# One core: batch 0's narrowing steps signalled singly from GpSimd, and a new order of the work on four engines

## The chip, the cores and the metric

One core of a Trainium2 chip runs one launch of the kernel. The metric is the device time of the launch in microseconds, lower is better. The engines are TensorE (PE), VectorE (DVE), ScalarE (ACT), GpSimd (POOL) and SyncE (SP, which issues transfers); each takes its own queue of instructions in order, and they meet only at semaphores.

## The reference

```python
# x: (4, 256, 256), ctx_512: (4, 256, 64)
def attention(h, x_normed, Wq, Wk, gamma_raw):           # h = ctx_512
    sim = einsum('bhnd,bhmd->bnm', heads(h @ Wq.T), heads(h @ Wk.T)) / (sqrt(16) * 4)
    threshold = top_k(sim, 76)[0][:, :, -1:]             # 76 = int(256 * 0.3)
    A = sigmoid(sim) * (sim >= threshold)
    A = (A + swapaxes(A, -1, -2)) * 0.5
    gamma = sigmoid(gamma_raw)
    return (1 - gamma) * x_normed + gamma * A

def ffn(x):                                              # rows of 256, 8 experts, 2 a row
    w, idx = top_k(softmax(x @ gate_w.T), 2)
    y = sum over the two experts: w * ((silu(x @ w1.T) * (x @ w3.T)) @ w2.T)
    z = (silu(x @ ws1.T) * (x @ ws3.T)) @ ws2.T          # shared expert
    return y + z

x = x + attention(ctx_512, layernorm(x), Wq, Wk, gamma_raw)
x = x + ffn(layernorm(x))
```

All is float32. Every expert is computed for every row; the routing weight of an expert that a row does not take is zero.

## The kernel before

The four batches (b = 0 to 3) of 256 rows are handled one after the other as two tiles of 128 partitions. For each batch there is an attention part and an expert part, and the experts come in five slots: slot 0 is the shared expert, slots 1 to 4 hold two experts each. Weights and activations are split into a high and a low part, and each product is three passes (high by high, high weight by low, low by high).

The attention part of a batch: TensorE makes queries and keys (`project`, L1282) and the scores (`similar`, L1299). The 76th largest score of each row is narrowed down by counting: a pivot is guessed from mean and deviation, the scores above it are counted, and the pivot is moved by a step in proportion to the count, twice. For batch 0 the left column of tiles is narrowed by VectorE (`narrow0`, L909) and the right one by ScalarE (`lean_first`, `lean_second`, `lean_last`, L654 to L677); GpSimd makes the step sizes and start values (`spans0`, L384). For batches 1 to 3 GpSimd makes them (`steps`, L394) and ScalarE counts (`first_balance`, `second_balance`, `last_pivot`). Then VectorE counts once more (`count_above`), removes what is above (`drop_above`), takes the next 16 values (`take_near`), picks the threshold and masks (`select`, L989). GpSimd says for each row whether the threshold lies within the 16 (`find_hits`, L417), TensorE sums this (`sum_hits`, L1308) and VectorE reads it (`read_hits`). TensorE transposes the masked scores (`transpose_masked`, L1317), VectorE adds (`residual1`, L1046), and the second layer norm is `norm2` on GpSimd (L433), then `norm2_first` on VectorE for batch 0 or `normed2` on ScalarE for the others; `transpose_z` (TensorE), `high_z` (ScalarE) and `low_z` (VectorE) make the two halves of the normed rows.

The expert part of slot s: `up` (L1379, TensorE) into two PSUM banks in turn, `silu` (ScalarE), `gate_values` (VectorE), `gate` with the routing weights (GpSimd, L443), `high_g` (ScalarE), `low_g` (VectorE), `down` (TensorE). `logits`, `route_a`, `tanh_logits`, `route_b` give the routing weights, and SyncE spreads them over all partitions through memory (`spread_gates`, L310). `up_lo` and `dn_lo`, the low parts of the weights, are made once, in the time of batch 0, by `lower_up` and `lower_down`, on GpSimd or for slots 1 and 3 on VectorE.

`keep_warm(n)` (L1276) issues n products of a tile of ones on TensorE, whose result nobody reads; each leaves two records in the trace. They stand in TensorE's queue between steps of batch 0, so that step and filler run in the order written. The order of every engine's work is written out by hand at the end of its block (L489 to L542 GpSimd, L726 to L820 ScalarE, L1168 to L1272 VectorE, L1454 to L1529 TensorE). Each engine stops at the first instruction whose semaphore is not there, whatever stands behind it.

## Time and profile before

| what | value |
|---|---|
| time, median of 3 runs | 113.38 us (113.3 to 114.48) |
| span of the profiled execution, first to last instruction | 111.5 us |
| median less that span | 1.88 us |
| TensorE busy | 102.9 us, 92% |
| VectorE busy | 84.4 us, 76% |
| GpSimd busy | 70.4 us, 63% |
| ScalarE busy | 61.7 us, 55% |
| share of TensorE in the chain that ended last | 78% |

The page of the profile gives the span of its own execution and no separate time for it; what lies around the span (start and end of the launch) is the third row of the table, if that execution was a middling one. Records of TensorE are pipelined, so the distance between the starts of two records says what one costs, and the length of one record is more than that. In a timeline, the note in brackets gives the idle time of the engine ahead of a row and who ended it; a row without one began as the engine came free.

### The profile page before, as it was taken

What the parts mean: (1) busy time and instruction counts of PE and PEld (TensorE: products, weight loads), DVE (VectorE), ACT (ScalarE), POOL (GpSimd) and SP (SyncE); (2) the same over time, 40 slices, a digit from 0 to 9 for tenths busy, and PEclk for the clock granted to TensorE, in tenths of its full rate; (3) what the DMA queues carried; (4) which work ended last, traced back from release to release, by engine and by line L of the source; (5) the groups of instructions that cost most, each with busy time, mean ns of one, the idle gap of its engine ahead of it and who ended that gap; (6) DMA issues with size and microseconds to landing.
All of it is one profiled execution on the core that took longest, in us unless ns stands there. A gap on an engine that the chain in (4) does not pass through costs nothing.

```text
span 111.5 us, 2502 instructions
## 1 busy us (share of the span) xinstructions
PE 102.9 (92%) x816; PEld 100.5 (90%) x816; DVE 84.4 (76%) x276; ACT 61.7 (55%) x155; POOL 70.4 (63%) x141
## 2 busy tenths in 40 slices
PE   6899709889999999999999999999999999999990
PEld 6699608778999999999999999999999999999990
DVE  6689899899998789867659979759418979365731
ACT  4179999989669856289691245243513352052400
POOL 4047788894975887899898591697028550465500
PEclk9999997699999999999999999999999999999999
DMA  2699995000003700000029000010483004520002
GB/s 40 135 341 370 343 374 163 3 0 3 0 0 96 281 9 0 3 0 6 3 47 309 21 9 0 32 62 0 111 263 104 6 3 154 228 94 0 0 0 94
DMA packets 8158, 10.33 MB, mean 93 GB/s; under 512 B 1936, under 2 KB 6544, under 8 KB 8144
## 3 DMA queue, kind: packets, MB, share of 16 engines
q1 hardware_dynamic: 7776, 10.13, 28.6%
q8 instruction: 6, 0.10, 0.4%
q10 hardware_dynamic: 368, 0.04, 0.3%
q14 instruction: 8, 0.07, 0.2%
HBM read 9.09 MB, written 1.08 MB: 91 GB/s over the span
## 4 chain that ended last, share of the span: by engine, by line
PE 78%; POOL 8%; DVE 5%; ACT 4%; issue 2%; POOLq 0%
PE ps_h L1407 23%; PE ps_u L1407 22%; PE ps_y L1435 20%; PE ps_a L1435 3%; PE ps_c L1354 3%; PE ps_u L1280 3%; ACT qkT L577 2%; PE ps_b L1337 1%; DVE near L970 1%; PE ps_a L1325 1%; PE ps_h L1289 1%; POOL rs L371 1%; DVE st L870 1%; DVE left L962 1%; DVE z L1060 1%
## 5 line engine op out<-in xcount | busy, mean ns | idle before, releaser
L452 POOL TENSOR_TENSOR gc<-prod,weights 128x512 f32<-128x512 f32 x16 | 25.9, 1634 | 15.3 <-DMA weights<-gates 9.3
L699 ACT ACTIVATE sil<-ps_h 128x512 f32<-128x512 f32 (+1 forms) x20 | 10.9, 552 | 16.1 <-PE ps_h L1407 16.1
L710 ACT ACTIVATE g_hi<-gc 128x512 fp32r<-128x512 f32 x16 | 10.1, 630 | 15.9 <-POOL gc L452 15.9
L1435 PE MATMUL ps_y<-dn_hi,g_hi 128*128 128x256 f32 x63 | 17.9, 284 | 0.0
L1435 PE MATMUL ps_y<-dn_hi,g_lo 128*128 128x256 f32 x63 | 17.7, 281 | 0.0
L1435 PE MATMUL ps_y<-dn_lo,g_hi 128*128 128x256 f32 x63 | 17.7, 281 | 0.0
L1136 DVE TENSOR_TENSOR g_lo<-gc,g_hi 128x512 fp32r<-128x512 f32 x16 | 13.8, 862 | 2.5 <-ACT g_hi L710 2.1
L1407 PE MATMUL ps_h<-z_hi,up_hi 128*128 128x256 f32 x70 | 14.7, 291 | 0.0
L1124 DVE TENSOR_TENSOR prod<-sil,ps_u 128x512 f32<-128x512 f32 x16 | 10.8, 679 | 4.9 <-ACT sil L699 3.2
L1407 PE MATMUL ps_h<-z_hi,up_lo 128*128 128x256 f32 x70 | 14.0, 281 | 0.0
L1407 PE MATMUL ps_u<-z_hi,up_hi 128*128 128x256 f32 x70 | 14.0, 281 | 0.0
L1407 PE MATMUL ps_h<-z_lo,up_hi 128*128 128x256 f32 x70 | 14.0, 281 | 0.0
L1407 PE MATMUL ps_u<-z_hi,up_lo 128*128 128x256 f32 x70 | 14.0, 281 | 0.0
L1407 PE MATMUL ps_u<-z_lo,up_hi 128*128 128x256 f32 x70 | 14.0, 281 | 0.0
L1280 PE MATMUL ps_u<-ones 128*128 128x128 f32 x72 | 12.5, 321 | 1.0 <-POOL ones L457 1.0
L1280 PEld LDWEIGHTS ps_u<-ones 128*128 128x128 f32 x72 | 11.8, 234 | 1.5 <-POOL ones L457 1.0
L1435 PEld LDWEIGHTS ps_y<-dn_lo,g_hi 128*128 128x128 f32 x63 | 11.9, 189 | 0.0
L1435 PEld LDWEIGHTS ps_y<-dn_hi,g_lo 128*128 128x128 f32 x63 | 11.9, 188 | 0.0
L1435 PEld LDWEIGHTS ps_y<-dn_hi,g_hi 128*128 128x128 f32 x63 | 11.9, 188 | 0.0
L1407 PEld LDWEIGHTS ps_h<-z_lo,up_hi 128*128 128x128 f32 x70 | 10.7, 188 | 0.0
L1407 PEld LDWEIGHTS ps_u<-z_lo,up_hi 128*128 128x128 f32 x70 | 10.7, 188 | 0.0
L1407 PEld LDWEIGHTS ps_u<-z_hi,up_lo 128*128 128x128 f32 x70 | 10.7, 188 | 0.0
(210 smaller groups left out, 250.3 us busy)
## 6 DMA issues: line engine op xcount, KB each, us to landing
weights<-gates SPq DMA_DIRECT2D x8, 512.0 KB, 4.5
x_sb<-in_x SPq DMA_DIRECT2D x4, 256.0 KB, 6.0
up_raw<-in_w1t SPq DMA_DIRECT2D x4, 256.0 KB, 5.9
up_raw<-in_w3t SPq DMA_DIRECT2D x4, 256.0 KB, 6.0
dn_raw<-in_w2t SPq DMA_DIRECT2D x4, 256.0 KB, 6.2
out_x<-fin SPq DMA_DIRECT2D x3, 256.0 KB, 2.1
out_x<-fin SPq DMA_DIRECT2D x2, 128.0 KB, 1.7
ctx_sb<-in_ctxT SPq DMA_DIRECT2D x1, 192.0 KB, 4.6
```

Of the source, the lines that this page charges most:

```text
L371: link(nc.gpsimd.tensor_tensor(rs1[:, :], var1[:, :], minus_half[:, :], ALU.pow))
L452: nc.gpsimd.tensor_tensor(gc[k % 2][:, :].rearrange("p (n t q) -> p n t q", n=2, t=T), prod[s][:, :].rearrange("p (n t q) -> p n t q", n=2 ...
L577: nc.scalar.activation(qkT[b][0:DC, a, :], ps_qk[b][a * DC:(a + 1) * DC, 0:N], ACT.Copy)\
L699: nc.scalar.activation(sil[i % 2][:, :w], ps_h[i % 2][:, :w], ACT.Silu).then_inc(silu_ready, 1)
L710: nc.scalar.activation(g_hi[s][:, :], src[:, :], ACT.Copy).then_inc(ghi0_ready if s == 0 else ghi_ready, 1)
L870: nc.vector.bn_stats(st0[0][:, t, :], ps_first[t][:, 0:N]).then_inc(first_stats, 1)
L1124: nc.vector.tensor_tensor(dst[:, :w], sil[i % 2][:, :w], ps_u[i % 2][:, :w], ALU.mult).then_inc(prod_ready, 1)
L1136: nc.vector.tensor_tensor(g_lo[s][:, :], src[:, :], g_hi[s][:, :].bitcast(F32), ALU.subtract).then_inc(glo0_ready if s == 0 else glo_ready, 1)
L1280: nc.tensor.matmul(ps_u[1][:, 0:P], ones[:, :], ones[:, :], start=True, stop=True)
L1354: last = nc.tensor.matmul(ps_c[:, t * 2 * E:(t + 1) * 2 * E], zz[b % 2][:, k, t * P:(t + 1) * P], gate_r[:, k, :, :].rearrange("p a e -> p ...
L1407: last = nc.tensor.matmul(dst, w[:, e, a, k, :], zz[b % 2][:, k, :], start=(m == 0), stop=(m == 3 * KD - 1))
L1435: last = nc.tensor.matmul(dst[:, t * D:(t + 1) * D], g[s][:, tok], w[:, e, :], start=(s == 0 and first and m == 0), stop=(s == SLOTS - 1 a ...
```

## The change

GpSimd's `spans0` issues the shift of the first step ahead of everything else, and each of three results raises `span_ready` by one: `from_a`, `from_b`, `step_b`. VectorE and ScalarE wait for the count that they need at each use, where before they waited once for the whole. Beside it the written order of all four engines is new. VectorE does both narrowing steps ahead of `gamma_parts` and `norm1(1)`; after `add_masked0` it takes `residual1(0)`, `score_stats(2)` and `norm2_first` ahead of `lower_up(1, 0)`. GpSimd does `lower_up(0, 1)`, `norm2(0)`, `steps(2)` and `find_hits(1)` ahead of `lower_down(0)` and `lower_gate`, and puts `lower_up(4, 0)` and `(4, 1)` ahead of `norm2(1)`. TensorE does `similar(3)` early, has longer stretches of `keep_warm` on either side of `transpose_masked(0)`, and takes `sum_hits(1)` behind `up(0, 1)`. A wait for `fin_ready` is put into `residual1(3)`. The diff, with later parts of the orders left out:

```diff
@@ -384,12 +385,14 @@
             def spans0():
 
                 pool.wait_ge(dev0_ready, 1)
+                nc.gpsimd.tensor_tensor(shifted_a[:, :], dev[0][:, :], shift_a[:, :], ALU.mult).then_inc(shifted_ready, 1)
                 nc.gpsimd.tensor_tensor(step_a[:, :], dev[0][:, :], scale_a[:, :], ALU.mult)
-                nc.gpsimd.tensor_tensor(step_b[:, :], dev[0][:, :], scale_b[:, :], ALU.mult)
-                nc.gpsimd.tensor_tensor(shifted_a[:, :], dev[0][:, :], shift_a[:, :], ALU.mult)
-                link(nc.gpsimd.tensor_tensor(shifted_b[:, :], dev[0][:, :], shift_b[:, :], ALU.mult))
-                nc.gpsimd.tensor_tensor(from_a[:, :], shifted_a[:, :], mv0[0][:, :, 0], ALU.add)
+                nc.gpsimd.tensor_tensor(shifted_b[:, :], dev[0][:, :], shift_b[:, :], ALU.mult).then_inc(shifted_ready, 1)
+                pool.wait_ge(shifted_ready, 1)
+                nc.gpsimd.tensor_tensor(from_a[:, :], shifted_a[:, :], mv0[0][:, :, 0], ALU.add).then_inc(span_ready, 1)
+                pool.wait_ge(shifted_ready, 2)
                 nc.gpsimd.tensor_tensor(from_b[:, :], shifted_b[:, :], mv0[0][:, :, 0], ALU.add).then_inc(span_ready, 1)
+                nc.gpsimd.tensor_tensor(step_b[:, :], dev[0][:, :], scale_b[:, :], ALU.mult).then_inc(span_ready, 1)
...
@@ -499,39 +502,39 @@
             find_hits(0)
             steps(1)
             norm1(1)
+            lower_up(0, 1)
+            norm2(0)
+            steps(2)
+            find_hits(1)
+            lower_up(2, 0)
+            lower_up(2, 1)
             lower_down(0)
             lower_gate()
-            norm2(0)
-            find_hits(1)
-            lower_up(0, 1)
-            lower_up(2, 0)
-            lower_up(2, 1)
             add_masked(1)
-            steps(2)
-            norm2(1)
             lower_up(4, 0)
             lower_up(4, 1)
+            norm2(1)
             norm1(2)
+            lower_down(1)
+            steps(3)
+            find_hits(2)
             gate(0, 1)
-            find_hits(2)
             gate(0, 2)
-            gate(0, 3)
-            steps(3)
             add_masked(2)
-            lower_down(1)
             lower_down(2)
             norm2(2)
+            gate(0, 3)
             gate(0, 4)
             lower_down(3)
...
@@ -663,6 +666,7 @@
                 act.wait_ge(span_ready, 1)
                 nc.scalar.activation(aim1[:, 1:2], lean[:, 0:1], ACT.Identity, bias=from_a[:, 1:2],
                                      scale=step_a[:, 1:2]).then_inc(lean_aim_ready, 1)
+                act.wait_ge(span_ready, 2)
                 nc.scalar.activation(part0[:, 1:2], lean[:, 0:1], ACT.Identity, bias=from_b[:, 1:2],
                                      scale=step_a[:, 1:2]).then_inc(lean_part_ready, 1)
...
+                act.wait_ge(span_ready, 3)
                 nc.scalar.activation(pivot[0][:, 1:2], lean[:, 1:2], ACT.Identity, bias=part0[:, 1:2],
                                      scale=step_b[:, 1:2]).then_inc(lean_pivot_ready, 1)
...
@@ -725,9 +730,9 @@
 
             copy_q0()
             tanh_first()
+            tanh_gamma()
             copy_qk(1)
             copy_qk(2)
-            tanh_gamma()
             lean_first()
             copy_qk(3)
             lean_second()
@@ -735,81 +740,81 @@
             lean_last()
             copy_scores_summed()
             sigmoid(0)
-            upper_down(0)
-            sigmoid(1)
             upper_up(0, 1)
-            upper_gate()
             upper_up(1, 0)
             upper_up(1, 1)
+            copy_scores(2)
+            upper_down(0)
             first_balance(1)
             second_balance(1)
             last_pivot(1)
-            copy_scores(2)
-            upper_down(1)
+            copy_scores(3)
+            upper_gate()
+            high_z(0)
             upper_up(2, 0)
             upper_up(2, 1)
             upper_up(3, 0)
-            high_z(0)
-            copy_scores(3)
+            silu(0, 0)
...
@@ -913,12 +918,14 @@
                     dve.wait_ge(tanh_ready, 1)
                     link(count_first(0, aim0))
                     dve.wait_ge(span_ready, 1)
-                    nc.vector.tensor_scalar(part0[:, 0:1], count[:, 0:1], step_a[:, 0:1], from_b[:, 0:1],
+                    nc.vector.tensor_scalar(aim1[:, 0:1], count[:, 0:1], step_a[:, 0:1], from_a[:, 0:1],
                                             ALU.mult, ALU.add)
-                    link(nc.vector.tensor_scalar(aim1[:, 0:1], count[:, 0:1], step_a[:, 0:1], from_a[:, 0:1],
+                    dve.wait_ge(span_ready, 2)
+                    link(nc.vector.tensor_scalar(part0[:, 0:1], count[:, 0:1], step_a[:, 0:1], from_b[:, 0:1],
                                                  ALU.mult, ALU.add))
                 else:
                     link(count_first(0, aim1))
+                    dve.wait_ge(span_ready, 3)
                     link(nc.vector.tensor_scalar(pivot[0][:, 0:1], count[:, 0:1], step_b[:, 0:1], part0[:, 0:1],
                                                  ALU.mult, ALU.add))
 
...
                 dve.wait_ge(maskT_ready, b + 1)
                 dve.wait_ge(base_ready, b + 1)
+                if b >= 3:
+                    dve.wait_ge(fin_ready, T * (b - 2))
                 nc.vector.tensor_tensor(x1[b % 3][:, :, :], base[:, :, :],
                                         ps_a[:, :].rearrange("p (t n) -> p t n", t=T), ALU.add).then_inc(x1_ready, 1)
...
@@ -1170,10 +1179,10 @@
             first_score_stats()
             norm1(0)
             aims0()
+            narrow0(0)
+            narrow0(1)
+            gamma_parts()
             norm1(1)
-            narrow0(0)
-            gamma_parts()
-            narrow0(1)
             count_last0(0)
             count_last0(1)
             drop_above(0)
@@ -1182,88 +1191,88 @@
             take_near(0, 1)
             select(0)
             add_masked0()
+            residual1(0)
+            score_stats(2)
+            norm2_first()
             lower_up(1, 0)
-            residual1(0)
+            count_above(1)
+            low_z(0)
             lower_up(1, 1)
-            count_above(1)
-            norm2_first()
             drop_above(1)
             take_near(1, 0)
+            gate_values(0, 0)
             take_near(1, 1)
+            lower_up(3, 0)
+            gate_values(0, 1)
             read_hits(1)
-            low_z(0)
             select(1)
-            score_stats(2)
-            route_a(0)
-            gate_values(0, 0)
-            residual1(1)
-            low_g(0, 0)
-            route_b(0)
-            gate_values(0, 1)
-            lower_up(3, 0)
             lower_up(3, 1)
             norm1(2)
+            gate_values(0, 2)
+            residual1(1)
+            route_a(0)
+            route_b(0)
+            low_g(0, 0)
+            score_stats(3)
+            gate_values(0, 3)
             low_z(1)
-            gate_values(0, 2)
-            score_stats(3)
-            route_a(1)
-            gate_values(0, 3)
+            gate_values(0, 4)
             count_above(2)
-            gate_values(0, 4)
             drop_above(2)
             take_near(2, 0)
             gate_values(1, 0)
-            low_g(0, 1)
+            norm1(3)
             take_near(2, 1)
             read_hits(2)
...
@@ -1458,64 +1467,60 @@
             keep_warm(1)
             project(1)
             project(2)
+            project(3)
             keep_warm(1)
-            project(3)
-            keep_warm(6)
             similar(1)
             similar(2)
+            similar(3)
             keep_warm(7)
             sum_hits(0)
-            keep_warm(2)
+            keep_warm(15)
             transpose_masked(0)
-            keep_warm(1)
-            similar(3)
-            keep_warm(7)
-            sum_hits(1)
-            keep_warm(1)
+            keep_warm(16)
             transpose_z(0)
             keep_warm(3)
             up(0, 0)
+            up(0, 1)
+            sum_hits(1)
+            up(0, 2)
             logits(0)
-            keep_warm(1)
             transpose_masked(1)
-            up(0, 1)
-            up(0, 2)
+            up(0, 3)
+            up(0, 4)
+            transpose_z(1)
             down(0, 0)
-            transpose_z(1)
-            up(0, 3)
+            up(1, 0)
             logits(1)
-            up(0, 4)
-            up(1, 0)
             up(1, 1)
             sum_hits(2)
             up(1, 2)
             transpose_masked(2)
             up(1, 3)
-            down(0, 1)
             up(1, 4)
             transpose_z(2)
+            down(0, 1)
...
```

## Rows read from the trace of the kernel before

**Rows 1.** Windows view: busy time of each engine, granted clock, DMA, by stretch.
```profile
18.00:19.00 1.00, 1.00 (x4) 0.81 (x3) 0.98 (x2) 1.00 (x5) 0.85 (x3) 0.50 0.06 19
...
26.10:60.00 33.90, 33.88 (x289) 33.88 (x290) 27.61 (x105) 25.02 (x64) 27.38 (x51) 1.00 0.16 46
60.00:109.00 49.00, 48.95 (x415) 48.75 (x414) 34.08 (x94) 15.77 (x30) 25.35 (x25) 1.00 0.22 73
```

**Rows 2.** Timeline of TensorE, 0 to 36 us: start, length, line, out<-in, count.
```profile
7.80 1.50 PE L1280 MATMUL ps_u<-ones 128*128 128x128 f32 x12
9.13 1.03 PE L1304 MATMUL ps_b<-qkT 128*128 128x256 f32 x4
...
13.52 0.69 PE L1280 MATMUL ps_u<-ones 128*128 128x128 f32 x4
16.97 0.63 PE L1325 MATMUL ps_a<-ident,masked 128*128 128x128 f32 x4 [2.76 <-DVE looked L1035]
...
19.12 2.77 PE L1280 MATMUL ps_u<-ones 128*128 128x128 f32 x14
22.82 0.35 PE L1314 MATMUL ps_a<-hit,ones 128*128 128x2 f32 x2 [0.93 <-POOL hit L424]
...
23.34 0.60 PE L1337 MATMUL ps_b<-ident,z 128*128 128x128 f32 x4
...
24.63 0.51 PE L1374 MATMUL ps_h<-z_hi,up_hi 128*128 128x256 f32 x2
...
26.12 0.51 PE L1374 MATMUL ps_h<-z_lo,up_hi 128*128 128x256 f32 x2 [0.28 <-DVE z_lo L1066]
```

**Rows 3.** Timeline of ScalarE, 0 to 45 us.
```profile
11.28 0.37 ACT L676 ACTIVATE pivot<-lean,part,step_b 128x1 f32<-128x1 f32 x1
...
20.39 0.63 ACT L584 ACTIVATE scores<-ps_h 128x256 f32<-128x256 f32 x2
```

**Rows 4.** Timeline of VectorE, 0 to 45 us.
```profile
11.69 0.48 DVE L906 TENSOR_SCALAR_CACHE_REDUCE over<-ps_y,pivot 128x256 f32<-128x256 f32 x1 [0.43 <-ACT pivot L676]
...
17.70 0.68 DVE L859 TENSOR_TENSOR up_lo<-up_raw,up_hi 128x512 fp32r<-128x512 f32 x1
18.30 0.68 DVE L1050 TENSOR_TENSOR x<-base,ps_a 128x512 f32<-128x512 f32 x1
...
19.80 0.25 DVE L839 BATCH_NORM_AGGREGATE mv<-st 128x2 f32<-128x6 f32 x2
...
21.84 0.74 DVE L1060 TENSOR_SCALAR z<-x,mv,rs 128x256 f32<-128x256 f32 x2 [0.36 <-POOL rs L437]
```

**Rows 5.** Timeline of GpSimd, 0 to 60 us, batch 0.
```profile
8.73 0.20 POOL L392 TENSOR_TENSOR from_b<-shifted_b,mv 128x2 f32<-128x2 f32 x1
...
19.95 0.76 POOL L364 TENSOR_TENSOR gate_r<-gate_sb,gate_r 128x16 fp32r<-128x16 f32 x1
...
21.09 0.71 POOL L437 TENSOR_TENSOR rs<-var,minus_half 128x2 f32<-128x2 f32 x1
```

**Rows 6.** Chain that ended last, 26 to 36 us: start, length, what.
```profile
28.41 1.42 PE ps_h L1407 x12
```

**Rows 7.** Timeline of GpSimd, 0 to 60 us, batch 1's second norm and what stands near it.
```profile
27.48 1.29 POOL L430 TENSOR_TENSOR base<-ln,masked 128x512 f32<-128x512 f32 x1 [1.64 <-DVE looked L1035]
...
31.39 0.33 POOL L435 TENSOR_SCALAR var<-mv 128x2 f32<-128x2 f32 x1
...
34.84 2.55 POOL L351 TENSOR_TENSOR up_lo<-up_raw,up_hi 128x512 fp32r<-128x512 f32 x2 [1.73 <-ACT up_hi L555]
```

**Rows 8.** Timeline of ScalarE, 0 to 45 us, batch 1's normed rows.
```profile
33.14 1.09 ACT L683 ACTIVATE z<-x,nb,rs 128x256 f32<-128x256 f32 x2 [0.18 <-POOL nb L441]
```

**Rows 9.** Timelines of GpSimd (0 to 60 us) and of VectorE (44 to 112 us).
```profile
45.01 1.61 POOL L452 TENSOR_TENSOR gc<-prod,weights 128x512 f32<-128x512 f32 x1 [1.06 <-DVE g_lo L1136]
...
46.36 0.31 DVE L975 SCALAR_TENSOR_TENSOR kth_pick<-above,count,near 128x16 f32<-128x16 f32 x1
...
46.60 0.22 DVE L975 SCALAR_TENSOR_TENSOR kth_pick<-above,count,near 128x16 f32<-128x16 f32 x1
```

More of the change, by code:

```diff
@@ L532, in _ @@
             gate(1, 3)
+            norm2(3)
             gate(1, 4)
-            norm2(3)
             gate(2, 1)
@@ L1215, in _ @@
             gate_values(1, 0)
-            low_g(0, 1)
+            norm1(3)
             take_near(2, 1)
@@ L1222, in _ @@
             residual1(2)
+            route_a(1)
             route_b(1)
+            low_g(0, 1)
             low_g(0, 2)
+            low_z(2)
+            count_above(3)
             gate_values(1, 3)
-            low_z(2)
-            norm1(3)
             gate_values(1, 4)
+            drop_above(3)
+            take_near(3, 0)
             low_g(1, 0)
             low_g(0, 3)
+            gate_values(2, 0)
+            low_g(0, 4)
             route_a(2)
-            count_above(3)
-            low_g(0, 4)
-            drop_above(3)
-            take_near(3, 0)
-            gate_values(2, 0)
-            gate_values(2, 1)
-            take_near(3, 1)
-            low_g(1, 1)
-            read_hits(3)
-            low_g(1, 2)
-            select(3)
-            residual2(0)
+            take_near(3, 1)
+            read_hits(3)
+            residual2(0)
+            select(3)
+            low_g(1, 1)
+            gate_values(2, 1)
             gate_values(2, 2)
             residual1(3)
+            low_g(1, 2)
+            route_b(2)
+            low_z(3)
             low_g(1, 3)
-            route_b(2)
+            gate_values(2, 3)
             low_g(1, 4)
-            gate_values(2, 3)
+            route_a(3)
             gate_values(2, 4)
-            low_z(3)
+            residual2(1)
             low_g(2, 0)
-            residual2(1)
             gate_values(3, 0)
-            route_a(3)
+            route_b(3)
             low_g(2, 1)
-            route_b(3)
             low_g(2, 2)
@@ L1260, in _ @@
             low_g(2, 4)
+            low_g(3, 0)
             gate_values(3, 1)
-            low_g(3, 0)
             gate_values(3, 2)
-            residual2(2)
             low_g(3, 1)
             low_g(3, 2)
+            residual2(2)
             gate_values(3, 3)
@@ L1493, in _ @@
             up(1, 3)
-            down(0, 1)
             up(1, 4)
             transpose_z(2)
+            down(0, 1)
             down(0, 2)
+            logits(2)
             up(2, 0)
-            logits(2)
             up(2, 1)
```

77 lines of the change are left out of this document (39 added, 38 removed).

## The prediction

> **What bounds the kernel now.** I read the windows first, because the busy shares of the whole span hide two different stages. From 26.1 to 109 us TensorE is busy in all but 0.07 of 82.9 us at the full clock [rows 1]: there nothing but TensorE's own work counts, as long as the other engines keep ahead of it. So a change of order can win only by letting that stretch begin sooner, and it can lose by opening holes in it. Next the timeline of TensorE shows what the stretch waited for [rows 2]. The transposes of batch 0's normed rows start at 23.34, the first product of `up(0, 0)` at 24.63, and its third pass at 26.12, behind `low_z(0)`. Last come the timelines of the engines that feed these three points [rows 3 to 5].
>
> **The narrowing, signalled singly.** Before, the single signal comes with `from_b` at 8.93 [rows 5]; now `from_a` signals ahead of it, by a few tenths. VectorE also does its two narrowing steps ahead of `norm1(1)`. But both columns have to be there before the scores of batch 0 are sorted out, and the right column belongs to ScalarE: VectorE sat idle for 0.43 us ahead of its count of that column, and ScalarE's pivot at 11.28 to 11.65 ended the wait [rows 3, 4]. ScalarE came to that pivot without an idle note, so it was late by its own queue; up to there the change only moves `tanh_gamma` in it, and the sum in front of the first lean count stays. VectorE's work ahead of that point is the same set in another order, so the 0.43 us cover the delay of `norm1(1)`; without them it would cost up to that. I book nothing, with bounds of -0.1 and +0.1 for two more waits in ScalarE's queue. The new wait in `residual1(3)` is for `residual2(0)`, earlier in VectorE's own queue: nothing.
>
> **Batch 0 from mask to normed rows.** Before, `lower_up(1, 0)` on VectorE, begun at 17.70 as `add_masked0` ended, kept `residual1(0)` back to 18.30 [rows 4]. It is now behind, so the residual starts near 17.72, as soon as the transposes are through (16.97 and 0.63 after it [rows 2]). From the residual's start to its last statistics took 20.05 - 18.30 = 1.75 us [rows 4], so these come at 19.47. On GpSimd `norm2(0)` began only once `lower_gate` ended at 20.71, and was done at 21.80 [rows 5]: 1.09 us. In the new order only `lower_up(0, 1)` stands ahead, in the place of `lower_down(0)` and of the same size, over about when `lower_gate` began, 19.95. I put `norm2(0)` at 19.75 to 19.95 and its end at 20.85 to 21.05, 0.75 to 0.95 us sooner. `norm2_first` took 0.74 [rows 4], so the normed rows are complete at 21.6 to 21.8; `score_stats(2)`, put in between, fills VectorE's wait.
>
> Before, this gain would have been lost: rows ready at 22.58 were transposed only at 23.34, since `sum_hits(1)` stood ahead in TensorE's queue and waited 0.93 us for GpSimd's hits [rows 2, 4]. That step now follows `up(0, 1)`. What stands ahead now is filler. A record of filler costs (9.13 - 7.80) / 12 = 0.111 us [rows 2]; 30 of them from 13.52 end at 16.85, just before the transposes of the mask (16.97). Four transposes and 32 records of filler more, at the same pitch, end at 20.97, before the rows are ready. So the filler is hidden, with 0.6 us to spare. `similar(3)`, moved early, is hidden too: TensorE idled between the early filler and the first hits.
>
> From the first of four transposes to `up(0, 0)` took 24.63 - 23.34 = 1.29 us; now two of the four are done while the second tile is normed, which saves 0.22. `up(0, 0)` starts at 21.6 + 1.07 = 22.67. ScalarE has both score copies of batches 2 and 3 ahead of `high_z(0)` now, about 1 us each by the two halves in [rows 3] and a tanh; they sit in its queue near 16 and 21, and I estimate that it is free at 21.7, before it is needed at 22.05. The third pass follows 26.12 - 24.63 - 0.28 = 1.21 us after the start, the wait taken off [rows 2], at 23.88. It needs `low_z(0)`: VectorE has `lower_up(1, 0)` and `count_above(1)` between, together 1.5 us (from 20.0, the end of the statistics, to 21.48, where the idle note of the 21.84 row begins [rows 4]); 21.55 + 1.5 + 0.68 for a product of 128x512 gives 23.7, or 0.3 later if GpSimd's `steps(2)` gets in between. So the third pass runs at 23.88 to 24.1 instead of 26.12: 2.0 to 2.25 us. One filler goes out of the full stretch and `sum_hits(1)` comes in, each two records: nothing. I take 2.25.
>
> **What the full stretch gives back.** Two places in the new order look too tight.
>
> First, `transpose_z(1)`. A pair of `up` costs 2.84 us (twice the piece in [rows 6]). TensorE has up(0, 0) done at 24.4, two pairs, a sum, the logits and the mask's transposes till 31.7, then two pairs, and wants batch 1's normed rows at 37.3. `residual1(1)` cannot start before 31.8. With 1.75 us for it and 34.23 - 31.39 = 2.84 us from GpSimd's `norm2(1)` to the end of ScalarE's rows [rows 7, 8] they could be there at 36.4. But GpSimd now has `add_masked(1)` (1.29) and `lower_up(4, 0)` and `(4, 1)` (2.55 [rows 7]) ahead of `norm2(1)`. If these begin only with the mask, near 31.0, `norm2(1)` starts at 34.8 and the rows end at 37.7; if a microsecond later, at 38.7. The stall is 0 to 1.4, and I take 0.3, near the first case.
>
> Second, `select(2)`. `gate(0, 2)` now stands immediately ahead of `add_masked(2)` on GpSimd, which waits for `select(2)`, and batch 0's routing weights come later, as `route_b(0)` moved behind `residual1(1)`. So GpSimd's two long products (1.61 us each) fall on the time when VectorE picks the threshold of batch 2, with small instructions that read two operands. The first `kth_pick` at 46.36, begun while a gate ran to 46.62, took 0.31 and not 0.22 [rows 9]. So the price lies between nothing and one whole gate, 1.6 us; how the two meet I can place only to a microsecond. I take 0.6, nearer the row, which lost 0.09. The Trainium skill, page "SBUF — State Buffer", section "Who interferes with whom", says that a VectorE instruction with two SBUF inputs contends with a GpSimd instruction that reads SBUF, and that the later one blocks until the other is through. The row agrees, since only the last 0.26 us of the gate were left; taken at the row's 0.09 this place would leave the time at 111.5, by the rule at its worst at 113.0. It reaches TensorE whole, since `transpose_masked(2)` stands in its queue with `up(1, 3)` behind.
>
> Sum: 2.25 - 0.3 - 0.6 = 1.35 us. The span goes from 111.5 to 110.15; with the same 1.88 around it, 112.0 against the median of 113.38.
>
> **Rivals.** (a) No hole opens: 113.38 - 2.25 = 111.1. For it speak the slack that the other engines have (VectorE is busy 27.6 of 33.9 us, GpSimd 27.4 [rows 1]); against it, both places above. (b) The holes eat the gain: both at the upper bound, 1.4 + 1.6 = 3.0, gives 114.1; the middle of both, 1.5, gives 112.6, and a third hole of half a microsecond in a queue where every order is new gives 113.1. For it: GpSimd's chain from the mask to the normed rows of batch 1 is longer by two products. (c) Slower: the filler runs at half clock. From 18 to 19 the granted clock was 0.50, the 1.2 GHz level, after TensorE had idled 2.76 us [rows 1, 2], and 14 records took 2.77 us, 0.198 each. The new filler lies on the path. If only the second block (32 records) runs so, it ends 2.8 us later, at 23.8, and `up(0, 0)` starts at about 25: near no change. If the clock falls before the mask's transposes, 30 records more cost 2.6 us and the third pass comes at about 29.2: 116.4. Whether the clock falls before 16.97 decides. Against it: the idle time ahead that let it fall is filled. (d) The change misses its own aim, since the narrowing's gain ends at ScalarE: that is in my sum already, and costs nothing.
>
> **How the numbers follow.** Of changes here, 1% (1.1 us) is about what a measurement tells from none. The forecast, holes of some 0.5 to 1.1 us in all: 0.37. (a): 0.19. (b): 0.33, within 1% for nearly all. (c) slow: 0.07, and 0.04 for holes above 3.4 us. So faster 0.56, same 0.33, slower 0.11. The range of the likeliest alone is 111.7 to 112.3; with (a) below it and (b) up to 113.9 it is 110.9 to 113.9, which leaves out (c) and a lucky start.
>
> **What would show it.** VectorE still waits for ScalarE's pivot near 11.65; `norm2_first` near 20.9 and `up(0, 0)` near 22.7, with the third pass on its heels; granted clock 1.00 from 13 to 21; TensorE's waits list a normed row or a copy of batch 1 near 37 and the mask of batch 2 near 47, a few tenths each; the end of TensorE's work about 1.35 us sooner. I am wrong if `up(0, 0)` starts at 24 or later, if the holes sum to over 1.5 us, or if filler is what TensorE ends last before a transpose.

## The result: 0.6% faster, half of what was forecast

The changed kernel takes 113.32 us in the median of 20 executions (112.47 to 114.84) against 113.56 us for the kernel before (113.3 to 114.5, 20 executions). The ratio is 0.9943, 95% interval 0.9918 to 0.9969: 0.65 us less of 113.56, with 0.35 to 0.93 inside the interval. The ratio leaves out the five longest executions of the changed kernel (114.32 us and above) as slow ones, which is one reason why it says more than the two medians; over all 20 the means are 113.50 and 113.78, 0.28 us apart. The forecast was 1.35 us less, so the time falls into "within 1%". The direction is right and the size is not.

Four views show where the 0.65 us come from. First the windows of the changed kernel, with the columns of [rows 1]; the second one begins with the third pass of `up(0, 0)`:

```profile
18.00:19.00 1.00, 1.00 (x11) 0.98 (x11) 0.89 (x3) 1.00 (x6) 0.92 (x2) 1.00 0.12 43
25.02:60.00 34.98, 34.62 (x288) 33.65 (x287) 31.84 (x118) 26.81 (x67) 28.39 (x46) 1.00 0.09 32
```

The granted clock at 18 to 19 us, 0.50 before [rows 1], is now 1.00. But the full stretch, idle for 0.02 us of 33.9 before [rows 1], now has 34.98 - 34.62 = 0.36 us of idle time in its first half (none from 60 to 109). Records of TensorE that wait for an operand also count as busy, so the timeline shows more (start, length, line, out<-in, count; compare [rows 2]):

```profile
18.07 0.63 PE L1334 MATMUL ps_a<-ident,masked 128*128 128x128 f32 x4
18.54 3.74 PE L1289 MATMUL ps_u<-ones 128*128 128x128 f32 x32
22.61 0.67 PE L1346 MATMUL ps_b<-ident,z 128*128 128x128 f32 x4 [0.34 <-DVE z L1069]
...
25.02 0.39 PE L1383 MATMUL ps_h<-z_lo,up_hi 128*128 128x256 f32 x2
...
38.39 0.84 PE L1346 MATMUL ps_b<-ident,z 128*128 128x128 f32 x4
39.00 0.36 PE L1444 MATMUL ps_y<-dn_hi,g_hi 128*128 128x256 f32 x1
...
39.92 0.50 PE L1416 MATMUL ps_h<-z_hi,up_hi 128*128 128x256 f32 x2
...
40.64 0.51 PE L1416 MATMUL ps_h<-z_lo,up_hi 128*128 128x256 f32 x2
...
49.02 0.63 PE L1334 MATMUL ps_a<-ident,masked 128*128 128x128 f32 x4 [0.36 <-DVE looked L1042]
49.61 0.47 PE L1416 MATMUL ps_h<-z_hi,up_hi 128*128 128x256 f32 x2
```

The last two rows have these for counterparts in the kernel before:

```profile
48.97 0.60 PE L1325 MATMUL ps_a<-ident,masked 128*128 128x128 f32 x4
49.32 0.48 PE L1407 MATMUL ps_h<-z_hi,up_hi 128*128 128x256 f32 x2
```

The reader is to see three things. The filler is out of the way before each group of transposes: what ends the wait at 22.61 is VectorE's normed row, and at 18.07, where no wait is noted, the transposes follow VectorE's last step of the mask by 0.22 us (17.85), as they do in e6 with a third of the filler. The third pass stands at 25.02, not at 23.88 as forecast. And the two holes are there, each where it was expected. At 38.39 the transposes of batch 1 take 0.61 us to the next start, where batch 3's, unstalled, took 0.36 (76.50 to 76.86), and the passes at 39.92 and 40.64 are late as well. At 49.02 the mask of batch 2 is waited for, and the step behind its transposes comes after 0.59 us, where it came after 0.35 before.

The timelines of VectorE and GpSimd in the same execution, which answer to [rows 4, 5, 7]:

```profile
9.70 0.27 DVE L921 TENSOR_SCALAR aim<-count,step_a,from_a 128x1 f32<-128x1 f32 x1
...
12.78 0.48 DVE L911 TENSOR_SCALAR_CACHE_REDUCE over<-ps_y,pivot 128x256 f32<-128x256 f32 x1 [0.23 <-ACT pivot L681]
...
22.06 0.73 DVE L1069 TENSOR_SCALAR z<-x,mv,rs 128x256 f32<-128x256 f32 x2 [0.39 <-POOL rs L440]
...
29.79 0.20 DVE L993 TENSOR_SCALAR hits<-ps_a 1x1 int32<-1x1 f32 x1
...
30.74 0.88 DVE L987 SCALAR_TENSOR_TENSOR masked<-scores,kth,sig 128x256 f32<-128x256 f32 x2 [0.45 <-DVE kth_pick L982]
...
35.17 0.25 DVE L844 BATCH_NORM_AGGREGATE mv<-st 128x2 f32<-128x6 f32 x2
...
46.22 1.56 DVE L982 SCALAR_TENSOR_TENSOR kth_pick<-above,count,near 128x16 f32<-128x16 f32 x1
...
48.78 0.68 DVE L1133 TENSOR_TENSOR prod<-sil,ps_u 128x512 f32<-128x512 f32 x1
...
81.27 0.95 DVE L1092 TENSOR_TENSOR lgd<-lgx,lg 128x16 f32<-128x16 f32 x1
82.15 0.15 DVE L1094 COPY take<-lg 128x4 f32<-128x4 f32 x1
```
```profile
33.34 2.57 POOL L352 TENSOR_TENSOR up_lo<-up_raw,up_hi 128x512 fp32r<-128x512 f32 x2
36.00 0.22 POOL L438 TENSOR_SCALAR var<-mv 128x2 f32<-128x2 f32 x1
...
44.49 3.25 POOL L455 TENSOR_TENSOR gc<-prod,weights 128x512 f32<-128x512 f32 x2
```

Batch 1's statistics were there at 35.42, but GpSimd's `norm2(1)` began at 36.00, behind the two products of `lower_up(4, *)`. The first `kth_pick` of batch 2 took 1.56 us (0.31 in [rows 9], and 0.22 for the second one there): it began during `gate(0, 2)` and ended with it, at 47.7. The row at 48.78 is `gate_values(1, 1)`, behind the masks in VectorE's queue.

For the comparison of several kernels I read the starts of a few steps from TensorE's timeline of each. The columns: from the first scores to the sum of batch 0's hits; from there to the third pass of `up(0, 0)`; from the transposes of batch 1's normed rows to its logits; from there to the mask transposes of batch 2; from there to batch 2's logits; from the logits of batch 3 to TensorE's end; from the third pass to the end (us; of before, whose order is another, the first two and the last).

| kernel | scores to hits | hits to pass | norm 1 to logits 1 | to mask 2 | to logits 2 | logits 3 to end | pass to end |
|---|---|---|---|---|---|---|---|
| before | 8.19 | 12.81 | | | | | 82.84 |
| changed | 9.13 | 10.62 | 3.31 | 7.32 | 9.62 | 29.45 | 84.21 |
| e1_same | 8.96 | 10.63 | 3.28 | 7.34 | 9.62 | 30.23 | 84.97 |
| e2_one_signal | 9.43 | 10.61 | 3.29 | 7.32 | 9.61 | 29.45 | 84.15 |
| e3_gate_behind | 9.10 | 10.62 | 3.29 | 6.79 | 10.18 | 29.45 | 84.27 |
| e4_read_early | 8.21 | 10.62 | 3.06 | 7.21 | 9.61 | 29.99 | 84.41 |
| e5_norm2_late | 8.54 | 11.31 | 3.29 | 7.38 | 9.62 | 29.45 | 84.27 |
| e6_little_filler | 8.88 | 11.06 | 3.30 | 7.36 | 9.61 | 29.64 | 84.53 |
| e7_batch3 | 8.19 | 10.62 | 3.28 | 7.36 | 9.61 | 29.45 | 84.19 |
| e8_best | 8.23 | 10.63 | 3.52 | 6.93 | 9.62 | 29.44 | 84.06 |
| e9_product_early | 8.20 | 10.64 | 3.06 | 7.72 | 9.62 | 29.45 | 84.34 |
| e11_two_edits | 8.19 | 10.62 | 3.06 | 7.16 | 9.61 | 29.45 | 83.78 |

The first column is not the change's: it differs between executions of one order (e4, e7 and e11 have the changed order up to there and 8.19 to 8.21, as before; the changed kernel itself 9.13 and 8.96). The second column is the gain, 12.81 - 10.62 = 2.19; it is 10.61 to 10.64 in every execution but those of e5 and e6, whose edits lie in it. The last is the loss, 84.21 - 82.84 = 1.37, and 2.13 in the second execution.

### The profile page after: what moved, and what is told of

Same layout as the page of the kernel before. It is cut to its first block, busy times and chain, and to the rows that moved or that the text cites. A ratio compares the mean times of both kernels' runs of the same rounds, so it can differ in the third digit from the quotient of the medians.

```text
span 111.8 us, 2555 instructions
## 1 busy us (share of the span) xinstructions
PE 106.6 (95%) x842; PEld 102.9 (92%) x842; DVE 83.0 (74%) x276; ACT 61.4 (55%) x155; POOL 71.9 (64%) x141
## 3 DMA queue, kind: packets, MB, share of 16 engines
HBM read 9.09 MB, written 1.08 MB: 91 GB/s over the span
## 4 chain that ended last, share of the span: by engine, by line
PE 74%; POOL 10%; DVE 8%; issue 5%; ACT 1%; DVEq 0%; POOLq 0%
PE ps_h L1416 20%; PE ps_y L1444 19%; PE ps_u L1416 19%; PE ps_a L1444 3%; PE ps_u L1289 3%; PE ps_c L1363 2%; PE ps_b L1346 2%; PE ps_a L1334 1%; POOL up_lo L352 1%; PE ps_h L1298 1%; PE ps_c L1305 1%; DVE near L977 1%; PE ps_h L1383 1%; DVE ps_b L900 1%; POOL rs L372 1%
## 5 line engine op out<-in xcount | busy, mean ns | idle before, releaser
L455 POOL TENSOR_TENSOR gc<-prod,weights 128x512 f32<-128x512 f32 x16 | 27.0, 1708 | 16.6 <-DMA weights<-gates 8.1
L1145 DVE TENSOR_TENSOR g_lo<-gc,g_hi 128x512 fp32r<-128x512 f32 x16 | 12.3, 781 | 8.2 <-ACT g_hi L715 8.1
L1289 PE MATMUL ps_u<-ones 128*128 128x128 f32 x98 | 13.9, 296 | 1.0 <-POOL ones L460 1.0
L1289 PEld LDWEIGHTS ps_u<-ones 128*128 128x128 f32 x98 | 13.4, 211 | 1.4 <-POOL ones L460 1.0
L1416 PEld LDWEIGHTS ps_h<-z_hi,up_hi 128*128 128x128 f32 x70 | 10.7, 189 | 0.3 <-ACT z_hi L696 0.2
L1416 PEld LDWEIGHTS ps_u<-z_hi,up_hi 128*128 128x128 f32 x70 | 10.7, 188 | 0.0
```

What stands on the lines that cost most here:

```text
L455: nc.gpsimd.tensor_tensor(gc[k % 2][:, :].rearrange("p (n t q) -> p n t q", n=2, t=T), prod[s][:, :].rearrange("p (n t q) -> p n t q", n=2 ...
L1145: nc.vector.tensor_tensor(g_lo[s][:, :], src[:, :], g_hi[s][:, :].bitcast(F32), ALU.subtract).then_inc(glo0_ready if s == 0 else glo_ready, 1)
L1289: nc.tensor.matmul(ps_u[1][:, 0:P], ones[:, :], ones[:, :], start=True, stop=True)
L1416: last = nc.tensor.matmul(dst, w[:, e, a, k, :], zz[b % 2][:, k, :], start=(m == 0), stop=(m == 3 * KD - 1))
```

## The experiments

Each is an edit of the changed kernel; the ratio is to the kernel before on the same chip. Only e5 and e10 have intervals clear of the unchanged order's 0.9918 to 0.9969, so what the other edits do is read from the rows and columns, with the ratio beside it.

**e1_same: the changed kernel once more.**

> The changed kernel once more, as it is, for a second trace. In the first trace the first scores of batch 0 took 1.19 us a pair where they took 0.67 before, and all of batch 0 came some 1.1 us late behind them. Theory: that is the clock of the first microseconds, which differs from execution to execution and not with the change. Then this trace may show the pair at 0.67 again, and if so the third pass of up(0, 0) comes at about 23.9, the span is about 110.7, and the holes near 38 to 41 us (0.5) and 48 to 50 us (0.6) stand as before, 1 us sooner. Rival: the new order makes the front late. Then the pair takes 1.19 again and the third pass comes at 25.0 again. Time against the kernel before: 0.990 to 0.997 by both.

Measured 113.5 us, ratio 0.995 (0.9917 to 0.9984): the result stands. Its trace shows a hole that the first one had not. VectorE, GpSimd and TensorE:

```profile
80.92 1.60 DVE L1092 TENSOR_TENSOR lgd<-lgx,lg 128x16 f32<-128x16 f32 x1
82.44 1.69 DVE L1094 COPY take<-lg 128x4 f32<-128x4 f32 x1
```
```profile
80.84 3.27 POOL L455 TENSOR_TENSOR gc<-prod,weights 128x512 f32<-128x512 f32 x2 [4.63 <-DMA weights<-gates]
```
```profile
85.28 0.47 PE L1416 MATMUL ps_h<-z_hi,up_hi 128*128 128x256 f32 x2 [0.54 <-DVE prod L1133]
```

`route_a(3)` on VectorE meets two of GpSimd's gates back to back. Here the first gate keeps `lgd` back for 1.60 us and the second one the copy for 1.69; in the execution above `lgd` took 0.95 and the copy got in between the gates, 0.15. `gate_values(2, 4)` stands behind, and TensorE's `up(3, 1)` waits for it. The hole is 30.23 - 29.45 = 0.78 us here, 0 in the other one.

**e2_one_signal: the old single signal in the new order.**

```diff
-  shifted_a.then_inc(shifted_ready) ... from_a.then_inc(span_ready), from_b.then_inc(span_ready), step_b.then_inc(span_ready)
+  step_a, step_b, shifted_a, link(shifted_b), from_a, from_b.then_inc(span_ready)      # and one wait for it
```

> The new order with the old signalling: spans0 signals once at its end, in its old sequence, and both narrowing engines wait for that. Theory: ScalarE's pivot ends the wait, VectorE had 0.23 us to spare in the changed kernel, and the single signal comes 0.3 to 0.45 later; so VectorE's last count comes at most 0.2 us later and the time is 0 to +0.2 us against the changed kernel, ratio to the kernel before 0.993 to 0.997. Rival: the single signals are what the change gains from; then the ratio is 1.00.

113.91 us, ratio 0.9988 (0.9954 to 1.0023). VectorE waits for the signal now:

```profile
10.04 0.27 DVE L916 TENSOR_SCALAR aim<-count,step_a,from_a 128x1 f32<-128x1 f32 x1 [0.54 <-POOL from_b L392]
```

It is at 10.04 where the changed kernel is at 9.70, 0.34 later with the scores 0.07 earlier. Everything behind in VectorE's queue is later too, `gamma_parts` with it, for which GpSimd waits ahead of the hits; the changed kernel and then this run (in the kernel before the wait was 0.18 us):

```profile
11.42 0.30 POOL L375 TENSOR_SCALAR c<-rs,g_rest 128x2 f32<-128x2 f32 x1 [0.43 <-DVE g_quarter L1174]
```
```profile
11.76 0.30 POOL L374 TENSOR_SCALAR c<-rs,g_rest 128x2 f32<-128x2 f32 x1 [0.73 <-DVE g_quarter L1167]
```

The first column is 9.43, against 8.88 to 9.13 in the four executions of the single signals whose first scores took as long. So in the new order the single signals are worth 0.3 us or more; the intervals of the two ratios overlap, and the rows carry this.

**e3_gate_behind: `gate(0, 2)` out of the pick's way.**

```diff
-  find_hits(2), gate(0, 1), gate(0, 2), add_masked(2)     # GpSimd
+  find_hits(2), gate(0, 1), add_masked(2), gate(0, 2)
-  gate_values(1, 2), residual1(2)                         # VectorE
+  residual1(2), gate_values(1, 2)
```

> gate(0, 2) behind add_masked(2) on GpSimd, and residual1(2) ahead of gate_values(1, 2) on VectorE. Theory: in the changed kernel the first pick of batch 2 took 1.56 us behind gate(0, 2) and TensorE stood 0.5 to 0.7 us for it. Without the gate there the pick takes 0.22, the hole near 49 us goes, and the time falls by 0.5 us against the changed kernel: ratio to the kernel before about 0.988 to 0.991. Rival: the hole is only moved, since gate(0, 2) and what waits for it come later; then the pick is short but the ratio stays at 0.994.

113.49 us, ratio 0.9948 (0.9913 to 0.9982): nothing gained. VectorE and GpSimd:

```profile
46.02 0.21 DVE L982 SCALAR_TENSOR_TENSOR kth_pick<-above,count,near 128x16 f32<-128x16 f32 x1
...
47.23 0.88 DVE L987 SCALAR_TENSOR_TENSOR masked<-scores,kth,sig 128x256 f32<-128x256 f32 x2 [0.83 <-DVE kth_pick L982]
```
```profile
49.55 1.65 POOL L455 TENSOR_TENSOR gc<-prod,weights 128x512 f32<-128x512 f32 x1
...
52.53 0.23 POOL L438 TENSOR_SCALAR var<-mv 128x2 f32<-128x2 f32 x1
```

The pick is free and the mask 0.53 us sooner (6.79 for 7.32), so the gate was what blocked it, and TensorE no longer waits for the mask. But `norm2(2)` now stands behind the gate, and batch 2's logits come 0.56 later: the hole has moved. The row at 47.23 shows a floor under it: between the sum of the hits at 45.90 and the masks lie 1.33 us, in which VectorE's queue reads the sum back for its branch.

**e4_read_early: the same read-back, for batch 1, ahead of a product.**

```diff
-  lower_up(3, 0), gate_values(0, 1), read_hits(1), select(1)     # VectorE
+  lower_up(3, 0), read_hits(1), gate_values(0, 1), select(1)
```

> read_hits(1) ahead of gate_values(0, 1) on VectorE, nothing else. Theory: in the changed kernel the masks of batch 1 began 0.95 us after read_hits(1) began, with 0.45 us of idle time, as they did for batch 2 in the kernel before, since the hits are read back into VectorE's queue; that kept add_masked(1), both lower_up(4) and norm2(1) on GpSimd late, which made the hole at 38 to 41 us. With the read 0.6 us earlier the idle time goes, norm2(1) comes 0.3 to 0.45 us sooner, that hole shrinks by 0.3: ratio to the kernel before about 0.991. Rival: norm2(1) is held by batch 1's own statistics on VectorE; then GpSimd waits for them and the hole stays.

113.05 us, ratio 0.9911 (0.9877 to 0.9945). In the changed kernel the masks of batch 1 come 0.95 us after `hits` with 0.45 of idle time; here the product of 0.67 lies in that time, the masks follow the picks with no wait, and the third column falls by 0.25. This execution has the hole of e1, the third one, at 0.54.

**e5_norm2_late: one product back ahead of batch 0's norm.**

```diff
-  lower_up(0, 1), norm2(0), ..., lower_up(2, 1), lower_down(0), lower_gate()     # GpSimd
+  lower_up(0, 1), lower_down(0), norm2(0), ..., lower_up(2, 1), lower_gate()
```

> The changed kernel with lower_down(0) put back ahead of norm2(0) on GpSimd, nothing else. My account of the front: norm2(0) ends the wait for batch 0's normed rows, so one product of 0.73 us ahead of it reaches TensorE whole: from the first scores to the third pass of up(0,0) 19.5 us at a cold first pair (18.8 at a warm one in the run with the early read) becomes 20.3 (19.6), and the ratio to the kernel before goes from 0.995 to 1.001. Rival: the front is bound by something else by now (the filler, ScalarE's copies, low_z), and the segment does not grow by more than 0.2 us.

114.24 us, ratio 1.0025 (0.9988 to 1.0062). TensorE waits for the normed row 0.70 longer, and the second column is 11.31 for 10.62, the 0.72 us of the product:

```profile
22.58 0.67 PE L1346 MATMUL ps_b<-ident,z 128*128 128x128 f32 x4 [1.04 <-DVE z L1069]
```

So what stands ahead of `norm2(0)` on GpSimd reaches TensorE one to one. The rest of the 2.19 us (`sum_hits(1)` out of TensorE's way, the residual ahead of `lower_up(1, 0)`) no run tested by itself.

**e6_little_filler: the filler cut from 31 products to 10.**

```diff
-  keep_warm(15), transpose_masked(0), keep_warm(16)     # TensorE
+  keep_warm(2),  transpose_masked(0), keep_warm(8)
```

> The changed kernel with 2 and 8 filler products for 15 and 16 ahead of and behind the transposes of batch 0's mask. If the filler is only cover, as the prediction had it, the clock falls as it did in the kernel before (0.50 at 18 to 19 us), but is back before up(0,0), and the third pass comes within 0.2 us of where it came. The rival: up(0,0) and the transposes ahead of it then run at half the clock, some 12 records at twice 0.12 to 0.24 us, and the third pass comes 0.5 to 1.5 us later; then part of the front's gain is the filler's, and the ratio is 1.000 to 1.008.

113.41 us, ratio 0.993 (0.9893 to 0.9967). The windows and the timeline of TensorE:

```profile
18.00:19.00 1.00, 1.00 (x7) 1.00 (x6) 0.69 (x3) 1.00 (x6) 0.90 (x2) 0.50 0.31 107
...
23.00:24.00 1.00, 1.00 (x9) 0.98 (x7) 0.88 (x5) 0.68 (x2) 0.86 (x6) 0.73 0.05 16
```
```profile
17.63 1.08 PE L1334 MATMUL ps_a<-ident,masked 128*128 128x128 f32 x4 [2.76 <-DVE looked L1042]
18.51 3.62 PE L1289 MATMUL ps_u<-ones 128*128 128x128 f32 x16
```

After 2.76 us without work the granted clock is 0.50, the 1.2 GHz level, until 23; 16 records of filler take as long as 32 did. It is back before `up(0, 0)`, so of the work that counts only the transposes run slowly (1.08 us for four, where they took 0.63 to 0.67): the third pass comes 11.06 - 10.62 = 0.44 us later, between what the two sides expected. In the time it is not to be seen beside the unchanged order.

**e7_batch3: the third hole taken away.**

```diff
-  route_a(3), gate_values(2, 4)     # VectorE
+  gate_values(2, 4), route_a(3)
-  high_g(2, 1), silu(2, 4)          # ScalarE
+  silu(2, 4), high_g(2, 1)
```

> The changed kernel with gate_values(2,4) ahead of route_a(3) on VectorE and silu(2,4) ahead of high_g(2,1) on ScalarE. The account of the third hole: it opens in some executions, when route_a(3)'s small products are blocked by two gates of GpSimd back to back and keep gate_values(2,4) back. Then here it never opens: from the logits of batch 3 to the end 29.45 us, and the time is below the unchanged order's by the hole's 0.5 to 0.8 times its frequency, 0.2 to 0.4 us: ratio 0.991 to 0.993. Rival: the blocked product then keeps back low_g or the weights of batch 3 and the hole comes later: 29.9 or more, ratio 0.995.

113.08 us, ratio 0.9933 (0.9899 to 0.9967), and no hole (29.45). In this trace the copy was not blocked (0.16), but it was in e8, e10 and e11, which have the same edit (1.65 to 1.69), and TensorE did not wait for `gate_values(2, 4)` in any of them. With the hole shut, the columns give 2.19 - 1.35 = 0.84 us, a ratio of 0.9926 beside 0.9933 measured; against the unchanged order the intervals overlap.

**e8_best: the first hole attacked at its cause.**

```diff
-  lower_up(2, 1), lower_down(0), lower_gate(), add_masked(1), lower_up(4, 0), lower_up(4, 1), norm2(1)     # GpSimd
+  lower_up(2, 1), lower_up(4, 0), lower_gate(), add_masked(1), lower_up(4, 1), lower_down(0), norm2(1)
-  norm1(2), gate_values(0, 2), residual1(1)                                                                # VectorE
+  gate_values(0, 2), residual1(1), norm1(2)           # with the edits of e4 and e7
```

> All that the runs so far point to: read_hits(1) ahead of gate_values(0,1), the reorder of batch 3, and for the first hole lower_up(4,0) ahead of add_masked(1) in the place of lower_down(0), which goes ahead of norm2(1), with norm1(2) behind residual1(1) on VectorE. If the holes are what GpSimd's and VectorE's orders make, the stretch from the second norm's transposes to the logits of batch 1 shrinks from 3.3 to 2.6 us, from the third pass to the end 83.3 to 83.6 us where the changed kernel has 84.2 to 85.0, and the ratio is 0.982 to 0.988. The rival: closing a hole lets the next wait come up, as in the run that moved a gate; then no more than the early read's 0.991.

113.09 us, ratio 0.9927 (0.9895 to 0.996): no better than without it. The rows of batch 1 are in time, and another wait has come up behind them, for a product that `norm1(2)` pushed back; the third column is 3.52.

```profile
39.30 0.48 PE L1416 MATMUL ps_h<-z_hi,up_hi 128*128 128x256 f32 x2 [0.57 <-DVE prod L1133]
```

**e9_product_early: that product ahead of `score_stats(3)`.**

```diff
-  low_g(0, 0), score_stats(3), gate_values(0, 3), low_z(1)     # VectorE, on top of e8
+  low_g(0, 0), gate_values(0, 3), low_z(1), score_stats(3)
```

> The version with all edits, and gate_values(0,3) and low_z(1) ahead of score_stats(3) on VectorE. In that version the first hole had moved from batch 1's normed rows to up(1,0)'s wait of 0.57 us for gate_values(0,3), which norm1(2) had pushed back. If that product is the last thing in the way, the stretch from the second transposes of normed rows to the logits of batch 1 falls from 3.52 to 2.6 to 2.8 us, from the third pass to the end 83.2 to 83.5 us (84.06 before the edit, 84.2 in the changed kernel), ratio 0.984 to 0.988. Rival: batch 1's z_lo or the later steps(3), which wait for score_stats(3), take its place: 83.9 or more, ratio 0.991 to 0.994.

113.36 us, ratio 0.9966 (0.9932 to 1.0): no better. The third column is 3.06, but the fourth is 7.72: TensorE now waits 0.77 us for the mask of batch 2. VectorE and TensorE:

```profile
38.58 0.69 DVE L1075 TENSOR_TENSOR z_lo<-ps_b,z_hi 128x512 fp32r<-128x512 f32 x1 [0.34 <-ACT z_hi L696]
...
45.82 1.02 DVE L982 SCALAR_TENSOR_TENSOR kth_pick<-above,count,near 128x16 f32<-128x16 f32 x1
...
47.04 0.88 DVE L987 SCALAR_TENSOR_TENSOR masked<-scores,kth,sig 128x256 f32<-128x256 f32 x2
```
```profile
48.09 0.63 PE L1334 MATMUL ps_a<-ident,masked 128*128 128x128 f32 x4 [0.77 <-DVE looked L1042]
```

With nothing left between the product and `low_z(1)`, VectorE stands still for 0.34 us, and no other idle time of it is noted until the masks; it reads the hits at 45.70, in e8 at 45.26, with the third pass at 23.96 in both. A gate blocks the pick here too, but that costs nothing: the masks begin 1.22 us after the pick began, as in e10 below, where the pick is free.

**e10_gate_later: `gate(0, 2)` behind `norm2(2)`.**

```diff
-  gate(0, 2), add_masked(2), lower_down(2), norm2(2)     # GpSimd, on top of e9
+  add_masked(2), lower_down(2), norm2(2), gate(0, 2)     # high_g, low_g, down (0, 2) moved along; residual1(2) ahead of gate_values(1, 2)
```

> The version with the earlier product, and gate(0,2) moved behind norm2(2) on GpSimd, with what hangs on it on ScalarE, VectorE and TensorE moved along (high_g(0,2), low_g(0,2), down(0,2)). In the run that moved gate(0,2) only behind add_masked(2), the pick was free (0.21 us) but batch 2's norm waited for the gate. If the second hole is only this one gate, then from the logits of batch 1 to the logits of batch 2 the time falls by 0.5 to 0.6 us against the version without the move, and the ratio is 0.979 to 0.985. Rival: the read-back of the hits (0.95 to 1.33 us from read_hits to the masks) or the late down(0,2) keeps 0.3 us or more of it.

121.5 us, ratio 1.0674 (1.0624 to 1.0724). I had overlooked a buffer: the product of slot 2 of batch 1 overwrites what `gate(0, 2)` reads, so VectorE stops at `gate_values(1, 2)`, and with it all behind it. VectorE from the pick on:

```profile
46.07 0.21 DVE L982 SCALAR_TENSOR_TENSOR kth_pick<-above,count,near 128x16 f32<-128x16 f32 x1
...
47.29 0.88 DVE L987 SCALAR_TENSOR_TENSOR masked<-scores,kth,sig 128x256 f32<-128x256 f32 x2 [0.84 <-DVE kth_pick L982]
...
54.83 0.69 DVE L1133 TENSOR_TENSOR prod<-sil,ps_u 128x512 f32<-128x512 f32 x1 [3.33 <-POOL gc L455]
```

Up to the masks the move gained nothing either: the pick took 0.21 us for 1.02, but the read-back of the hits lies beside it, and from the logits of batch 1 to the mask transposes it is 7.72 us, as in e9. What the second hole is worth when it is shut and nothing else opens is therefore not measured.

**e11_two_edits: the edits of e4 and e7, nothing else.**

> The changed kernel with the early read of batch 1's hits and the reorder of batch 3, nothing else. If the gains add up, 0.2 to 0.35 us from the first and 0.2 to 0.4 us on the average from the second (the hole that opens in some executions), the ratio is 0.988 to 0.990, from the third pass to the end 83.8 to 83.9 us. Rival: the two share one stall, and the ratio is 0.993 as for the batch 3 edit alone.

112.31 us against 113.56 in five executions, ratio 0.9899 (0.9863 to 0.9934), the lowest found. The interval still holds the rival's 0.993; the columns show the two gains side by side (3.06, 29.45, and 83.78 from the pass to the end). VectorE at `route_a(3)`; then ScalarE, VectorE and TensorE around `up(1, 0)`:

```profile
79.98 1.63 DVE L1092 TENSOR_TENSOR lgd<-lgx,lg 128x16 f32<-128x16 f32 x1
81.53 1.65 DVE L1094 COPY take<-lg 128x4 f32<-128x4 f32 x1
```
```profile
38.14 0.60 ACT L696 ACTIVATE z_hi<-ps_b 128x512 fp32r<-128x512 f32 x1 [0.25 <-PE ps_b L1346]
```
```profile
38.77 0.69 DVE L1075 TENSOR_TENSOR z_lo<-ps_b,z_hi 128x512 fp32r<-128x512 f32 x1 [0.55 <-ACT z_hi L696]
```
```profile
38.80 0.50 PE L1416 MATMUL ps_h<-z_hi,up_hi 128*128 128x256 f32 x2
...
39.52 0.51 PE L1416 MATMUL ps_h<-z_lo,up_hi 128*128 128x256 f32 x2
```

Both small instructions of `route_a(3)` are blocked in full, as in e1, and no hole follows (29.45), since the product that TensorE wants stands ahead of them, at 78.88. The first pass of `up(1, 0)` begins as `high_z(1)` ends, and the third as `low_z(1)` does.

## Why the prediction was right and wrong

**The narrowing, signalled singly: right in sum, by the luck of two terms that cancel.** ScalarE's pivot ends VectorE's last wait, as said (0.23 us at 12.78, 0.43 in [rows 4]), and scores to hits is 8.19 before and 8.19 to 8.23 in the executions with the same start. "I book nothing" hid that the new order of VectorE keeps `gamma_parts`, and so GpSimd, back, and that the single signals win it back, 0.3 us or more (e2).

**Batch 0 from mask to normed rows: right.** Forecast 2.0 to 2.25, taken 2.25; measured 2.19, and the third pass at 23.91 and 23.88 in e4 and e7 against 23.88 forecast. That VectorE waits for GpSimd's `norm2(0)` (row at 22.06) and that this place is worth what stands ahead of it was tested by e5. Rival (c) did not happen: the granted clock stayed at 1.00. e6 shows that the 21 products of filler that it lacks are worth at most 0.44 us.

**What the full stretch gives back: the step that failed.** "I take 0.3" and "I take 0.6", 0.9 together, and nothing for a third place; measured 0.60 and 0.77, together the 1.37 of the last column, and 0.22 more on the average. Each place was priced by the wait ahead of one group of transposes, and what stands behind that group was left out.

- First hole: the place and the lateness were right (`transpose_z(1)`, rows 0.25 us late where I took 0.3), the price was not. Unstalled, the stretch takes 0.36 (four transposes) + 0.79 (`down(0, 0)`, from 39.00 to 0.12 after its last start at 39.67) + 1.56 (`up(1, 0)` and the logits' start, 39.30 to 40.86 in e8) = 2.71; it took 3.31, 0.60 more. Late rows are 0.25 of it, and go with the early read (3.06). The other 0.35 stand also where the rows are in time, in e11: `high_z(1)` and `low_z(1)` come behind the transposes, and only `down(0, 0)` lies beside them.
- Second hole: the mechanism was right, and that the price came near is luck. The pick was blocked by the rest of the gate and took 1.56 us, 1.34 more than a free one; I took 0.6, nearer the row with 0.31, which showed only the end of a gate. And it does not reach TensorE "whole": the read-back of the hits, 0.95 to 1.34 us, lies beside it. Unstalled, the stretch to the mask takes 0.81 + 2.92 + 0.14 + 2.92 = 6.79 (logits from 41.70, `up(1, 1)` from 42.51, the sum from 45.43, `up(1, 2)` from 45.57), which is what e3 measured; it took 7.32, 0.53 more. Another 0.24 come behind the transposes (0.59 us for 0.35): `up(1, 3)` waits for `gate_values(1, 1)`, which stands behind the masks in VectorE's queue, ended at 49.46 and let it go at 49.61; in e3, e4, e8, e9 and e11 it also starts 0.15 us after that product ends. The Trainium skill ("SBUF — State Buffer", "Who interferes with whom") says that a VectorE instruction with two SBUF inputs contends with a GpSimd instruction that reads SBUF; the trace agrees, with 1.56 us, nearly a whole product of GpSimd (3.25 for the two at 44.49).
- Third hole: about half of the half microsecond of rival (b) "in a queue where every order is new", which had no place. It is `route_a(3)` against two gates: 0.78, 0.54 and 0.19 in three of the seven traces that have the changed order there (the changed kernel, e1 to e6), 0 in the others, on the average 0.22. The copy took 1.65 to 1.69 us in just these three, and 0.15 or 0.16 in the other four. It has one input; the same section of the Trainium skill says that a copy can enter a mode with two ports and then contend as well, and 1.69 us for 0.15 agree.

Sum: 2.19 - 0.60 - 0.77 - 0.22 = 0.60, beside 0.65 measured. So rival (b) came true: 113.38 less 0.65 is 112.7, inside its 112.6 to 113.1. By the sign that the prediction set itself, holes over 1.5 us in all, it was wrong as well: 1.37 in the execution above, 1.59 on the average.

**The median less the span** was 1.89 in the profiled execution (113.69 and 111.8), as assumed, but not in all: in five of the 20 executions of the changed kernel 2.67 to 3.24 us lie outside the span, in the others 1.77 to 1.93. The kernel before has 1.75 to 1.87 in all of the 84 executions beside the experiments. Over the fifteen executions in the ratio this comes to 0.14 us on the average, for which neither the prediction nor the sum above has a term; the cause is open.

## What to carry to other kernels

A gain ahead of a stretch in which one engine never waits is paid out only as far as the engines that feed it have slack at every place; sum the holes with the chain behind each late operand (copy, split, next product), not only its lateness. Small VectorE instructions of the kinds above cost up to a whole GpSimd product when that product is running (1.56 us for 0.22, 1.69 for 0.15): put what the bound engine waits for ahead of them, rather than move the GpSimd product. Most attempts to shut a hole by moving a large block opened the next one; the two edits that paid, by the columns, swapped neighbours.

## What the runs showed of the hardware that was not expected

**The start differs from execution to execution.** TensorE's first pair of scores took 1.19 us in the changed kernel and 0.67 in e7, whose queue is the same up to there:

```profile
5.27 1.19 PE L1305 MATMUL ps_c<-qkT 128*128 128x256 f32 x2 [0.18 <-DVE qkT L869]
```
```profile
5.07 0.67 PE L1305 MATMUL ps_c<-qkT 128*128 128x256 f32 x2 [0.39 <-DVE qkT L869]
```

The granted clock reads 1.00 from 5 to 7 us in both, yet these records take 1.8 times as long, and everything behind shifts by up to 1.1 us; why is open. It is as large as the effect under study and is why the profiled execution of the changed kernel is longer than that of before. The kernel before has one trace, with 0.67, so which of its stages differs cannot be told; its spans, 111.5 to 113.3 us in the 84 executions beside the experiments, spread as widely as the changed kernel's 110.6 to 112.7. The shortest of each are 0.9 us apart, near 2.19 - 1.37 = 0.82.

**Who goes first between two gates.** Between two gates back to back, a waiting VectorE copy gets in or does not: 0.15 or 0.16 us in six of the twelve traces with the new order (the changed kernel and e1 to e11), 1.65 to 1.69 in the other six, and differently in two executions of one program (the changed kernel and e1). Such a hole cannot be read from one trace.

**Reading a sum back into VectorE's queue** took 0.95 us (29.79 to 30.74), 1.33 us (45.90 to 47.23 in e3) and 1.34 us (45.95 to 47.29 in e10) to the next instruction that needs it; why it differs is open.
